# Where two of eight three-operand products stand in a graph kernel's second block

## The chip, the cores and the metric

The kernel runs on one core of a Trainium2 chip. The metric is the device time in microseconds (us) of one execution. The profile is one execution recorded by the hardware profiler; its times start at the first recorded instruction.

## The reference, cut to what matters

Four layers follow each other on 256 nodes of 512 features: a graph diffusion, a mixture of experts, a graph layer with 64 paths, and a second layer of experts. The change is in the third one, which works on 4352 edges:

```python
x1 = x_nodes[src].reshape(-1, N_SEG, EXTENT)          # 16 segments of 32
x2 = x_edges.reshape(-1, N_SEG, EXTENT)
i1, i2, i3 = (path_indices[:, 0], path_indices[:, 1], path_indices[:, 2])
contrib = path_coeffs[None, :, None] * x1[:, i1, :] * x2[:, i2, :]
edge_out = jnp.zeros(...).at[:, i3, :].add(contrib)
out = jnp.zeros((n_nodes, OP_SIZE), x_nodes.dtype).at[dst].add(edge_out.reshape(-1, OP_SIZE))
```

So each of 64 paths takes one segment of the gathered node rows, one segment of the edge rows and a coefficient, and adds the product to one segment of the edge's output. The outputs are then added up by target node.

## The kernel before

The 4352 edges lie as 34 tiles of 128, and they are taken in three blocks of 10, 14 and 10 tiles. In a block the 64 paths run one after the other. The running number of a path is n = 64 b + p, with b the block and p the path.

Each path passes three engines. ScalarE scales the path's edge segment by its coefficient into one of 12 slots (`scale(n)`, L595). VectorE multiplies the slot in place by the gathered node segment (`multiply(n)`, L1011). Then the slot is used up by two engines: TensorE adds the first tiles of it into PSUM (8 in the first block, 6 in the second, 4 in the third) by a matmul with the identity (L1326, L1329), and VectorE adds the remaining tiles into SBUF (`add(n)`, L1021). The counters are `scaled`, `mults`, `psums` and `sums`, in this order. A slot is written again 12 paths later, so `scale(n)` waits for `psums` and `sums` to reach n - 11.

The order on VectorE is written out by hand: multiply(n+1), add(n), multiply(n+2), and so on, over all three blocks without a break.

For paths with `direct(b, p)` true, which are paths 0 to 7 of the second block, ScalarE does nothing. VectorE makes the product out of three operands (segment of the node rows, coefficient, segment of the edge rows) with one `scalar_tensor_tensor` (L1006).

At the end of a block TensorE closes its PSUM banks (L1337, `block_ps`). ScalarE copies the eight banks of the first block out (`copy_sums`, L605 and L610, `block_out`), and TensorE opens them again for the next block, each when its copy is done (L1317, with two small matmuls, L1319, behind each). On ScalarE the copies of the first block stand in the queue ahead of its first work for the second block, which is scale(72).

TensorE also adds the finished tiles of the previous block into the nodes (`scatter`, L1273 and L1276), one tile after every sixth path of the second block. ScalarE makes the matrices for that (L573). After the last of these, ScalarE clears room for the third block (L627) and then scales its first paths.

GpSimd gathers the node rows of the third block by indirect DMAs, one per tile (L460). It waits until VectorE has made 64 products in all, then one product more for each third path. Their landings are counted in `row_in`, for which VectorE waits at the first product of a block.

Segment numbers are data. They lie packed in registers, and each engine computes a path's numbers from a word by a division and a remainder. At block changes words are moved to other registers (`moved`, `move_word`, L240).

Of the kernel before, what the change touches and what calls it, by code (L numbers as in the profile page):

```python
# [5 lines left out]
def graph_and_experts(nc, x, src, dst, edge, gnn_w, gnn_b, diff_w, wr, br, wgate, bgate,  # L6
# [37 lines left out]
    ROW_PATHS = -(-NP // 3)  # L44
# [8 lines left out]
    OWN_SLOTS, XN_SLOTS, PART_SLOTS = 5, 2, 3  # L53
    DR = 5
    BEHIND = 14
    DIRECT = [0, 8, 0]
    FREE_SLOTS = 2
    SPLIT = 8
    KEPT_AT = BLOCKS[2] - KEPT[2] - (BLOCKS[2] - SPLIT)
# [5 lines left out]
    with ExitStack() as ctx:  # L65
# [3 lines left out]
        def sem(name):  # L69
            return ctx.enter_context(nc.semaphore(name))  # L70
# [77 lines left out]
        def slot(n):  # L148
            return slots[n % SLOTS]

        def direct(b, p):

            return p < DIRECT[b]

        take = carve(big[:, :])
        w_sb = take([KC, D])
# [71 lines left out]
        def load_words(engine, lo, n):  # L228

            regs = [engine.alloc_register(f"{engine.engine.name}_word{load_words.made + i}") for i in range(n)]  # L230
            load_words.made += n
            engine.load(regs, path_w[0:1, lo:lo + n])
            return [engine.snap(r, donate=True, min_val=0, max_val=NS ** 6 - 1) for r in regs]
        load_words.made = 0

        def moved(engine, value, top):

            reg = engine.alloc_register(f"{engine.engine.name}_moved{load_words.made}")
            load_words.made += 1
            engine.reg_mov(reg, value)  # L240
            return engine.snap(reg, donate=True, min_val=0, max_val=top)

        def move_word(engine, words, i):
            words[i] = moved(engine, words[i], NS ** 6 - 1)
# [11 lines left out]
        def segment(ap, seg):  # L256

            b = ap.bitcast(mybir.dt.uint8).rearrange("p t (s u) -> p t s u", u=4 * U)
            return b[:, :, bass.ds(seg, 1), :].rearrange("p t o u -> p t (o u)").bitcast(mybir.dt.float32)

        def first_column(words, p):
            return column(words[p % ROW_PATHS], 2 * (p // ROW_PATHS))
# [4 lines left out]
        def single_column(words, p):  # L267
            return column(words[p // 6], p % 6)
# [13 lines left out]

        scatter_tile = {n: t for b in range(NB) for n, t in scatter_order(b)}
        split_tiles = [t for _, t in scatter_order(NB - 1)][BLOCKS[NB - 1] - SPLIT:]

        def gather_bank(t):
# [24 lines left out]
        edge_in = [sem(f"edge_in{b}") for b in range(NB)]  # L311
# [175 lines left out]
        def _(act):  # L487
# [67 lines left out]
            words = load_words(act, ROW_PATHS, COL_PATHS)  # L555
# [15 lines left out]
            def one_hot(n):  # L571
                act.wait_ge(scattered, n - DR + 1)
                nc.scalar.activation(dst_oh[:, n % DR, :], dst_ohb[:, scatter_tile[n], :], ACT.Copy).then_inc(dst_made, 1)  # L573

            def scattered_at(n):
                b = max(i for i in range(NB) if FIRST[i] <= n)
                return NP * (b + 1) + scatter_paths(b + 1)[n - FIRST[b]]

            def scale(n):
                b, p = n // NP, n % NP  # L580
                if p == DIRECT[b]:
                    act.wait_ge(edge_in[b], 16 if b < NB - 1 else 16 * (BLOCKS[b] // 2))
                if b and (p % 6 == 0 or p == DIRECT[b]):
                    move_word(act, words, p // 6)

                if n == FREE_SLOTS:
                    act.wait_ge(xn_out, 16 * H)
                if n == FREE_SLOTS + XN_SLOTS:
                    act.wait_ge(part_r, 2 * H)
                if n == OWN_SLOTS + XN_SLOTS:  # L590
                    act.wait_ge(gat_ps, PE_TILES)
                if n >= SLOTS:
                    act.wait_ge(psums, n + 1 - SLOTS)
                    act.wait_ge(sums, n + 1 - SLOTS)
                nc.scalar.activation(slot(n)[:, 0:BLOCKS[b], :],  # L595
                                     segment(edges[:, FIRST[b]:FIRST[b] + BLOCKS[b], :], single_column(words, p)),
                                     ACT.Copy, scale=coef_b[:, p:p + 1]).then_inc(scaled, 1)

            def copy_sums(b, lo, hi):
                if b >= 2:  # L600
                    act.wait_ge(scattered, FIRST[b - 1])
                for i, q in enumerate(sum_banks(b)[lo:hi], lo):
                    act.wait_ge(block_ps, banks_before(b) + i + 1)
                    if i < PT:
                        nc.scalar.activation(  # L605
                            kept_sums[b][:, 0:PT, i * P:(i + 1) * P].rearrange("p t (k u) -> p k t u", u=U),
                            bank[q].rearrange("p (k t u) -> p k t u", t=PT, u=U), ACT.Copy).then_inc(block_out, 1)
                    else:
                        w = D // PT2[b]
                        nc.scalar.activation(  # L610
                            kept_sums[b][:, PT:KEPT[b], (i - PT) * w:(i - PT + 1) * w].rearrange("p t (k u) -> p k t u", u=U),
                            bank[q].rearrange("p (k t u) -> p k t u", t=PT2[b], u=U), ACT.Copy).then_inc(block_out, 1)
# [3 lines left out]
            for n in range(FREE_SLOTS + XN_SLOTS):  # L616
                scale(n)
            for t in range(0, PE_TILES, 2):
                copy_gathered(t)
            for n in range(FREE_SLOTS + XN_SLOTS, NP * NB):  # L620
                b, p = n // NP, n % NP
                if b == 1 and p == 0:
                    copy_sums(0, 0, 8)
                if b == 2 and p == 0:
                    act.wait_ge(scattered, FIRST[1])
                    for i in range(BLOCKS[b] - KEPT[b]):
                        nc.scalar.activation(rest_sums[b][:, i, :], zero_b[:, 0:1].broadcast_to([P, D]), ACT.Copy)\  # L627
                            .then_inc(cleared[b], 1)
                for m in range(DR, T - SPLIT):
                    if scattered_at(m - DR) + BEHIND == n:  # L630
                        one_hot(m)
                if not direct(b, p):
                    scale(n)
                if b == 2 and p == LEAD - 1:
                    copy_sums(1, 0, PT)
                if b == 2 and p == REST_LEAD - 1:
                    copy_sums(1, PT, 8)
# [71 lines left out]
        def _(dve):  # L709
# [266 lines left out]

            nc.vector.memset(rest_sums[1][:, 0:4, :], 0.0).then_inc(cleared[1], 1)
            dve.wait_ge(packed, 3)
            words = [load_words(dve, 0, ROW_PATHS + -(-max(DIRECT) // 6))]
            for t in range(1, PE_TILES, 2):  # L980
                dve.wait_ge(gat_ps, t + 1)
                nc.vector.tensor_copy(x1g[0][:, t, :], gather_bank(t)).then_inc(gathered_odd, 1)  # L982
# [3 lines left out]
            def multiply(n):  # L986
                b, p = divmod(n, NP)
                if b and p < ROW_PATHS:
                    words[b][p] = moved(dve, words[b - 1][p], NS ** 6 - 1)
                if b and p % 6 == 0 and direct(b, p):  # L990
                    words[b][ROW_PATHS + p // 6] = moved(dve, words[b - 1][ROW_PATHS + p // 6], NS ** 6 - 1)
                tiles, xg = BLOCKS[b], x1g[b % 2]
                if p == 0:
                    if b == 0:
                        dve.wait_ge(gathered, PE_TILES // 2)
                        dve.wait_ge(row_in[b], 16 * (tiles - PE_TILES))
                    else:
                        dve.wait_ge(row_in[b], 16 * tiles)
                    if direct(b, 0):
                        dve.wait_ge(edge_in[b], 16)  # L1000
                v = slot(n)[:, 0:tiles, :]
                if direct(b, p):
                    if n >= SLOTS:
                        dve.wait_ge(psums, n + 1 - SLOTS)
                    i2 = single_column(words[b][ROW_PATHS:], p)
                    nc.vector.scalar_tensor_tensor(  # L1006
                        out=v, in0=segment(xg[:, 0:tiles, :], first_column(words[b], p)), scalar=coef_b[:, p:p + 1],
                        in1=segment(edges[:, FIRST[b]:FIRST[b] + tiles, :], i2), op0=ALU.mult, op1=ALU.mult).then_inc(mults, 1)
                    return
                dve.wait_ge(scaled, sum(not direct(*divmod(m, NP)) for m in range(n + 1)))  # L1010
                nc.vector.tensor_tensor(v, segment(xg[:, 0:tiles, :], first_column(words[b], p)), v, ALU.mult).then_inc(mults, 1)  # L1011

            def add(n):
# [7 lines left out]
                nc.vector.tensor_tensor(v, v, slot(n)[:, KEPT[b]:BLOCKS[b], :], ALU.add).then_inc(sums, 1)  # L1021

            multiply(0)
            for n in range(NP * NB):
                if n + 1 < NP * NB:
                    multiply(n + 1)
                add(n)
# [441 lines left out]
```

## Time and profile before

| | |
|---|---|
| three runs | 277.69, 277.73, 277.73 us; median 277.73 |
| the profiled execution | 277.7 us |
| its span | 275.9 us |
| granted TensorE clock in it | 1.00 of full speed |
| busy: TensorE matmul, VectorE, ScalarE, GpSimd | 96%, 82%, 60%, 23% of the span |

The span runs from the first to the last recorded instruction; 1.8 us of the execution's time lie around it. PE is TensorE's matmuls, PEld its weight loads, DVE VectorE, ACT ScalarE, POOL GpSimd. A q behind an engine's name is its sequencer, which handles register work. TensorE's busy share says little by itself, since overlapping matmuls that keep the engine warm are counted too.

### The profile page before, as it was taken

What the parts mean: (1) busy time and instruction counts of PE and PEld (TensorE: products, weight loads), DVE (VectorE), ACT (ScalarE), POOL (GpSimd) and SP (SyncE); (2) the same over time, 40 slices, a digit from 0 to 9 for tenths busy, and PEclk for the clock granted to TensorE, in tenths of its full rate; (3) what the DMA queues carried; (4) which work ended last, traced back from release to release, by engine and by line L of the source; (5) the groups of instructions that cost most, each with busy time, mean ns of one, the idle gap of its engine ahead of it and who ended that gap; (6) DMA issues with size and microseconds to landing.
All of it is one profiled execution on the core that took longest, in us unless ns stands there. A gap on an engine that the chain in (4) does not pass through costs nothing.

```text
span 275.9 us, 5689 instructions
## 1 busy us (share of the span) xinstructions
PE 265.6 (96%) x1651; PEld 186.7 (68%) x1660; DVE 224.9 (82%) x662; ACT 165.8 (60%) x336; POOL 63.1 (23%) x52
## 2 busy tenths in 40 slices
PE   6999999999999899999999999989999999999996
PEld 4666698886444799997778786756666664468633
DVE  5977565199657999999999999999999987855372
ACT  6920451011526999945788788499988819552260
POOL 4000060060006644304669991000000000000000
PEclk9999999999999999999999999999999999999999
DMA  5799990000014657733250002013544429000002
GB/s 186 242 412 410 442 406 17 0 2 1 1 38 128 179 137 254 223 119 86 66 131 26 2 1 76 4 24 150 159 151 148 154 86 349 27 0 2 2 0 76
DMA packets 12592, 33.91 MB, mean 123 GB/s; under 512 B 3345, under 2 KB 3602, under 8 KB 12306
## 3 DMA queue, kind: packets, MB, share of 16 engines
q1 hardware_dynamic: 10482, 26.73, 26.9%
q0 software_dynamic: 2080, 6.82, 8.6%
q8 instruction: 14, 0.23, 0.4%
q14 instruction: 16, 0.13, 0.2%
HBM read 32.50 MB, written 1.05 MB: 122 GB/s over the span
## 4 chain that ended last, share of the span: by engine, by line
PE 80%; DVE 9%; ACT 6%; issue 3%; DVEq 1%; DMA 1%; ACTq 0%; SPq 0%
PE psum L1326 15%; PE psum L1276 12%; PE psum L1230 10%; PE psum L1329 8%; PE psum L1254 5%; PE psum L1259 4%; PE psum L1402 3%; PE psum L1428 3%; PE psum L1173 3%; DVE big L1021 2%; PE psum L1159 2%; PE psum L1282 2%; PE psum L1317 2%; PE psum L1182 1%; PE psum L1440 1%
## 5 line engine op out<-in xcount | busy, mean ns | idle before, releaser
L460 POOL DMA_INDIRECT big<-xn_rows,big x26 | 51.3, 1974 | 54.5 <-DMA xn_rows<-xn 23.4
L595 ACT ACTIVATE prod<-edges,coef_b 128x320 f32 (+1 forms) x77 | 43.0, 593 | 10.1 <-PE psum L1329 8.4
L1276 PE MATMUL psum<-big,dst_oh 128*128 128x512 f32 x104 | 48.8, 593 | 0.0
L1011 DVE TENSOR_TENSOR prod<-big,prod 128x320 f32<-128x320 f32 (+1 forms) x77 | 40.5, 527 | 0.4 <-DVE big L982 0.2
L1326 PE MATMUL psum<-prod,ident 128*128 128x128 f32 x160 | 32.0, 294 | 0.6 <-DVE prod L1011 0.5
L1326 PEld LDWEIGHTS psum<-prod,ident 128*128 128x128 f32 x160 | 24.4, 190 | 10.0 <-issue 9.1
L1230 PE MATMUL psum<-edges,big 128*128 128x256 f32 x128 | 28.3, 380 | 0.0
L1276 PEld LDWEIGHTS psum<-big,dst_oh 128*128 128x128 f32 x104 | 18.0, 191 | 13.5 <-issue 13.4
L1230 PEld LDWEIGHTS psum<-edges,big 128*128 128x128 f32 x128 | 24.1, 190 | 3.5 <-issue 0.3
L1021 DVE TENSOR_TENSOR big<-big,prod 128x64 f32 (+2 forms) x80 | 26.3, 328 | 0.1
L595 ACT ACTIVATE xparts<-edges,coef_b 128x320 f32 (+1 forms) x45 | 24.2, 584 | 1.1 <-PE psum L1326 0.9
L1011 DVE TENSOR_TENSOR xparts<-big,xparts 128x320 f32<-128x320 f32 (+1 forms) x45 | 23.5, 523 | 0.3 <-ACT xn L595 0.3
L1329 PE MATMUL psum<-prod,ident 128*128 128x64 f32 (+1 forms) x110 | 19.8, 262 | 0.0
L1326 PE MATMUL psum<-xparts,ident 128*128 128x128 f32 x96 | 19.1, 294 | 0.7 <-DVE xparts L1011 0.7
L595 ACT ACTIVATE xn<-edges,coef_b 128x320 f32 (+1 forms) x32 | 17.6, 589 | 0.4 <-PE psum L1326 0.2
L551 ACT ACTIVATE edges<-psum 128x256 f32<-128x256 f32 x8 | 3.1, 384 | 24.2 <-PE psum L1230 18.6
L1011 DVE TENSOR_TENSOR xn<-big,xn 128x320 f32<-128x320 f32 (+1 forms) x32 | 16.8, 525 | 0.3 <-issue 0.2
L1329 PEld LDWEIGHTS psum<-prod,ident 128*128 128x128 f32 x110 | 16.7, 192 | 0.0
L595 ACT ACTIVATE src_t<-edges,coef_b 128x320 f32 (+1 forms) x30 | 16.3, 581 | 0.6 <-PE psum L1326 0.6
L1326 PEld LDWEIGHTS psum<-xparts,ident 128*128 128x128 f32 x96 | 14.1, 190 | 2.9 <-issue 2.6
L1021 DVE TENSOR_TENSOR big<-big,xparts 128x192 f32 (+2 forms) x48 | 15.9, 331 | 0.2 <-issue 0.2
L1011 DVE TENSOR_TENSOR src_t<-big,src_t 128x320 f32<-128x320 f32 (+1 forms) x30 | 15.6, 519 | 0.0
(217 smaller groups left out, 501.1 us busy)
## 6 DMA issues: line engine op xcount, KB each, us to landing
big<-in_w SPq DMA_DIRECT2D x3, 2048.0 KB, 16.2
edges<-in_f SPq DMA_DIRECT2D x11, 512.0 KB, 3.5
edges<-in_edge SPq DMA_DIRECT2D x1, 3584.0 KB, 23.9
edges<-in_edge SPq DMA_DIRECT2D x1, 2560.0 KB, 23.7
edges<-in_edge SPq DMA_DIRECT2D x5, 512.0 KB, 4.2
edges<-in_f SPq DMA_DIRECT2D x1, 2560.0 KB, 10.2
big<-in_gnn_w SPq DMA_DIRECT2D x1, 1024.0 KB, 6.3
xs<-in_x SPq DMA_DIRECT2D x1, 512.0 KB, 3.8
```

The lines of the kernel that those rows point to most:

```text
L460: nc.gpsimd.indirect_dma_start(out=x1g[b % 2][:, i, :], out_offset=None, in_=xn_rows, in_offset=bass.IndirectOffsetOnAxis(ap=idx_i[:, 0, F ...
L595: nc.scalar.activation(slot(n)[:, 0:BLOCKS[b], :], segment(edges[:, FIRST[b]:FIRST[b] + BLOCKS[b], :], single_column(words, p)), ACT.Copy, ...
L1011: nc.vector.tensor_tensor(v, segment(xg[:, 0:tiles, :], first_column(words[b], p)), v, ALU.mult).then_inc(mults, 1)
L1021: nc.vector.tensor_tensor(v, v, slot(n)[:, KEPT[b]:BLOCKS[b], :], ALU.add).then_inc(sums, 1)
L1173: last = mm(bank[2 + h], xnT[:, kc, h * P:(h + 1) * P], w_sb[:, kc, :], start=kc == 0, stop=kc == KC - 1)
L1230: last = mm(bank[2 + c % 4][:, n * N:(n + 1) * N], w[:, kc, c * P:(c + 1) * P], xnT[:, kc, :], start=kc == 0, stop=kc == KC - 1)
L1254: last = mm(bank[2 + h], hT[:, c, h * P:(h + 1) * P], w2_sb[:, c, :], start=c == 0, stop=c == HC - 1)
L1259: last = mm(gather_bank(t), src_t[:, h, t * P:(t + 1) * P], xparts[:, k, h, :], start=h == 0 and k == 0, stop=h == H - 1 and k == 2)
L1276: last = mm(bank[2 + h], dst_oh[:, n % DR, h * P:(h + 1) * P], tile_sums(b, t), start=False, stop=False)
L1326: last = mm(path_sums(to), ident[:], product[:, 0:PT].rearrange("p t u -> p (t u)"), start=False, stop=False, skip_group_check=True)
L1329: last = mm(more_sums(b, to), ident[:], product[:, PT:KEPT[b]].rearrange("p t u -> p (t u)"), start=False, stop=False, skip_group_check=True)
L1402: last = mm(bank[2 + k][64 * j:64 * j + 64, i * P:(i + 1) * P], yT[:, kc, c, :], f1_sb[:, kc, c * P:(c + 1) * P], start=k > 0 and kc == 0, ...
```

## The change

Paths 0 to 5 of the second block are no longer direct: ScalarE scales them and VectorE multiplies with two operands. Paths 6 and 7 stay direct. ScalarE's copies of the first block's sums move behind the scales of paths 0 to 5, so that its order is scale(63), scale(64) to scale(69), the eight copies, scale(72). The wait for the edge rows of the second block stands ahead of scale(64) on ScalarE and ahead of path 6 on VectorE.

```diff
-    DIRECT = [0, 8, 0]
+    DIRECT_LO, DIRECT_HI = 6, 8
 
         def direct(b, p):
 
-            return p < DIRECT[b]
+            return b == 1 and DIRECT_LO <= p < DIRECT_HI
 
             def scale(n):
                 b, p = n // NP, n % NP
-                if p == DIRECT[b]:
+                if p == 0:
                     act.wait_ge(edge_in[b], 16 if b < NB - 1 else 16 * (BLOCKS[b] // 2))
-                if b and (p % 6 == 0 or p == DIRECT[b]):
+                if b and (p % 6 == 0 or b == 1 and p == DIRECT_HI):
                     move_word(act, words, p // 6)
 
             for n in range(FREE_SLOTS + XN_SLOTS, NP * NB):
                 b, p = n // NP, n % NP
-                if b == 1 and p == 0:
+                if b == 1 and p == DIRECT_LO:
                     copy_sums(0, 0, 8)
 
-            words = [load_words(dve, 0, ROW_PATHS + -(-max(DIRECT) // 6))]
+            words = [load_words(dve, 0, ROW_PATHS + -(-DIRECT_HI // 6))]
 
-                    if direct(b, 0):
-                        dve.wait_ge(edge_in[b], 16)
                 v = slot(n)[:, 0:tiles, :]
                 if direct(b, p):
+                    if p == DIRECT_LO:
+                        dve.wait_ge(edge_in[b], 16)
                     if n >= SLOTS:
                         dve.wait_ge(psums, n + 1 - SLOTS)
```

## Rows read from the trace of the kernel before

**Rows 1.** Windows of VectorE: stretch, time, busy time (count), clock, DMA

```profile
133.31:182.37 49.06, 48.95 (x114) 1.00 0.14 38
182.37:226.00 43.63, 43.15 (x129) 1.00 0.41 137
```

**Rows 2.** Timeline, VectorE, at the first block change: start, length, engine, line, operation

```profile
125.16 0.21 DVE L1021 TENSOR_TENSOR big<-big,prod 128x64 f32 x1
125.29 0.48 DVE L1011 TENSOR_TENSOR xn<-big,xn 128x320 f32<-128x320 f32 x1
125.70 0.21 DVE L1021 TENSOR_TENSOR big<-big,xn 128x64 f32 x1
126.05 0.69 DVE L1006 SCALAR_TENSOR_TENSOR prod<-big,coef_b,edges 128x448 f32 x1
```

**Rows 3.** The same timeline through the direct paths and behind them

```profile
126.79 0.68 DVE L1006 SCALAR_TENSOR_TENSOR prod<-big,coef_b,edges 128x448 f32 x1
...
133.31 0.61 DVE L1011 TENSOR_TENSOR prod<-big,prod 128x448 f32<-128x448 f32 x1
...
137.67 0.61 DVE L1011 TENSOR_TENSOR prod<-big,prod 128x448 f32<-128x448 f32 x1
138.35 0.43 DVE L1021 TENSOR_TENSOR big<-big,prod 128x256 f32 x1
...
163.96 0.61 DVE L1011 TENSOR_TENSOR src_t<-big,src_t 128x448 f32<-128x448 f32 x1
164.60 0.43 DVE L1021 TENSOR_TENSOR big<-big,src_t 128x256 f32 x1
```

**Rows 4.** VectorE's sequencer by line: count, ns min/median/max, first and last start

```profile
L1011 DVEq FUSED_REGOPS  x184: 93/140/164, 90.4 to 225.1; - x184
L1006 DVEq FUSED_REGOPS  x8: 178/210/242, 125.8 to 131.9; - x8
```

**Rows 5.** Timeline, ScalarE, at the first block change

```profile
120.43 0.56 ACT L595 ACTIVATE xn<-edges,coef_b 128x320 f32 x1 [0.15 <-PE psum L1329]
126.94 2.07 ACT L605 ACTIVATE big<-psum 128x512 f32<-128x512 f32 x4 [5.94 <-remote]
130.78 1.29 ACT L595 ACTIVATE prod<-edges,coef_b 128x448 f32 x2
```

**Rows 6.** Timeline, TensorE: last path of the first block, an early scatter, three late ones

```profile
126.30 0.39 PE L1329 MATMUL psum<-xn,ident 128*128 128x128 f32 x2
138.08 1.88 PE L1276 MATMUL psum<-big,dst_oh 128*128 128x512 f32 x4
165.47 1.88 PE L1276 MATMUL psum<-big,dst_oh 128*128 128x512 f32 x4
170.75 1.88 PE L1276 MATMUL psum<-big,dst_oh 128*128 128x512 f32 x4
175.98 1.88 PE L1276 MATMUL psum<-big,dst_oh 128*128 128x512 f32 x4
```

**Rows 7.** Timeline, ScalarE and VectorE, at the second block change

```profile
177.90 3.22 ACT L627 ACTIVATE big<-zero_b 128x512 f32<-128x512 bf16 x6 [3.13 <-PE psum L1276]
181.03 1.00 ACT L595 ACTIVATE xparts<-edges,coef_b 128x320 f32 x2
182.37 0.49 DVE L1011 TENSOR_TENSOR xparts<-big,xparts 128x320 f32<-128x320 f32 x1
```

**Rows 8.** Timeline, GpSimd: four of the ten gathers for the third block

```profile
128.67 0.95 POOL L460 DMA_INDIRECT big<-xn_rows,big  x1 [0.38 <-DVE prod L1006]
134.19 4.91 POOL L460 DMA_INDIRECT big<-xn_rows,big  x1 [1.79 <-DVE prod L1011]
144.81 20.58 POOL L460 DMA_INDIRECT big<-xn_rows,big  x1 [1.19 <-DVE prod L1011]
165.69 1.03 POOL L460 DMA_INDIRECT big<-xn_rows,big  x1 [0.30 <-DVE prod L1011]
```

**Rows 9.** The gathers' line by itself: time from issue to landing

```profile
DMA to landing us min/median/max: 3.5/3.7/5.3
```

## The prediction

> **What bounds the kernel now.** The page's busy shares come first, and they mislead here: TensorE is busy for 96% of the span, and the chain that ended last goes through it over most of the path loops. So I read the windows of VectorE next. From the first two-operand product of the second block to the first product of the third it is busy for 48.95 of 49.06 us, and from there to the end of the loops for 43.15 of 43.63 us [rows 1]. Its timeline shows no wait for another engine in these two stretches. TensorE by itself is faster: in the second block its scatters, one in six paths, start 4.56 us apart while it has a backlog (27.39 us for six of them, from 138.08 to 165.47) [rows 6], and VectorE's six paths last 6 x 0.872 = 5.23 us [rows 3]. TensorE begins the block late and so looks full, but it has caught up by the scatter at 170.75, which comes 5.28 us after the one before, 0.72 us later than TensorE's own pitch would have it. From there it waits for VectorE. So VectorE's queue sets the time from 125.3 us to the end of the loops at 226 us, and behind that the tail runs as one serial chain. What shortens VectorE's queue anywhere in the second block is worth its full length, up to the 0.72 us that TensorE has in hand at that scatter.
>
> **The change part by part.** *Six products with two operands.* The direct product at 126.79 and the two-operand one at 133.31 are seven paths apart, 6.52 us or 0.931 us a path. The two-operand products at 133.31 and 137.67 are five paths apart, 4.36 us or 0.872 us a path [rows 3]. Both pitches hold the same addition. Six paths change: 6 x 0.059 = 0.355 us less. This is the main term. Paths 6 and 7 stay as they are.
>
> The Trainium skill ("VectorE: DVE Perf Modes", section "The TRN2 errata — SBUF-src ops pay a fixed extra latency per instruction") gives VectorE's time by a fixed part and the element count alone; by that both forms would last the same and this term would be nothing. The trace differs: 0.68 us against 0.61 us for the same 128x448 [rows 3]. The measurement decides, and the rule has no chance of its own.
>
> *The head of the block.* In the first block a product starts 0.13 us after the start of the addition ahead of it (125.16 to 125.29). The first product of the second block starts 0.35 us after it (125.70 to 126.05), so 0.22 us are lost there [rows 2]. The engine has no wait on another one; it is the sequencer, whose register work for a direct product lasts 210 ns against 140 ns for the other [rows 4], and which moves one word more. With a two-operand product first, 0.07 us of register work and the extra move go. Bounds: nothing, if the new wait for `scaled` takes as long as what it replaces, and the whole 0.22 us. I take 0.10, by the 0.07 us of the median rows and a little for the move. At path 6, where the move and the longer register work now stand, they have the 0.87 us of a product and an addition ahead of them as cover, as they had on the direct paths 1 to 7; uncovered they would cost the same 0.10 us again.
>
> *Six scales more on ScalarE.* It starts scale(63) at 120.43 us and then stands idle for 5.94 us until the copies at 126.94 [rows 5]. Scale(64+k) needs `psums` at 53+k. TensorE finishes path 63 at 126.30 + 0.39 = 126.7 us [rows 6], and one path each 0.54 us before that (125.16 to 125.70 on VectorE, which sets that pace) [rows 2]. So the last scale may start at 126.7 - 6 x 0.54 = 123.5 us and ends by 124.2, as two of them take 1.29 us [rows 5]. The first product that needs one is due at 126, and the first copy at 126.94. The cover is 2.7 us; if it were gone, each further 0.1 us would reach the copies, then TensorE's opening of the banks, and only beyond the 0.72 us of slack above the end. What is queued behind the new waits is the copies on ScalarE, and TensorE waits for these. Cost taken: nothing.
>
> *The wait for edge rows* moves to ScalarE at about 121 us. The transfers from outside that fill these rows are issued in the kernel's first 30 us, and VectorE finds them there at 126 without a wait [rows 2]; I take nothing, and no wait is added that anyone sees. The word moves on ScalarE are one register instruction more, in idle time: nothing.
>
> *What is queued behind.* All later steps are counted from VectorE's products: TensorE's last scatter of the second block (175.98), ScalarE's clearing behind it (177.90), scale(128) at 181.03, which VectorE needs at 182.37 [rows 6, 7]. These shift with VectorE, and so do the transfers that SyncE issues by `mults`. Scale(128) ends by 181.6, so there is 0.8 us of room as well. In the third block VectorE is idle for 0.48 us in 43.63 [rows 1], so nothing takes the gain up.
>
> *Sum.* 0.355 + 0.10 = 0.455 us. The profiled execution took 277.7 us, its span 275.9; that gives 277.25 us, and against the median of 277.73 it gives 277.3 us, a saving of 0.16%.
>
> **The rivals.** *Rival A: GpSimd is shut out, and the third block waits for its rows (slower).* Most gathers last 0.95 to 1.1 us, but two of those that start under VectorE's two-operand products of the second block last 4.91 and 20.58 us [rows 8]. Both begin after a wait for one of these products, and both end about 0.75 us after VectorE has a pause between a product and its addition: 138.35 stands 0.68 us behind its product, where the others have 0.53, and 164.60 is the second such place [rows 3]. The gather at 128.67, which waits for a direct product, lasts 0.95 us. After the change this one starts under two-operand products too, and may be held. A held gather costs nothing by itself: the last one is issued at 165.69 and lands 3.7 us later [rows 8, 9], and its rows are due at 182.0. It decides when a gather is still open behind the pause near 164 us and is then held until VectorE itself stops at the first product of the third block. Price: 0.75 us from the pause to the end of the issue and 3.7 us for the landing, 4.5 us, all of it on VectorE's full queue: 277.3 + 4.5 = 281.8 us; with two gathers open a further 1.3 us. Against it: each gather that followed straight after a held one got through, and the phases behind path 8 stay the same relative to VectorE. The Trainium skill ("SBUF — State Buffer", section "Who interferes with whom") says that a VectorE instruction with two SBUF inputs contends with a GpSimd instruction that reads SBUF; both product forms have two, so by it the change would add no exposure, while the rows above show a difference between places only.
>
> *Rival B: the time goes down by less than 0.1 us, or not at all.* VectorE has a pause of 0.1 to 0.2 us about every 30 paths, where its sequencer seems to fetch. The shorter code in front shifts the places of these pauses; if one lands where there is less cover, as in the first block's short additions or at the head of the second block, it takes up to 0.2 us, and the uncovered register work at path 6 the other 0.10: 277.45 to 277.75 us. For it speaks that the gain is so small; against it, that the pauses in the second block were 0.14 and 0.10 us and can hardly grow.
>
> *Rival C: more is gained.* The head's whole 0.22 us goes, and a pause is hidden: 0.355 + 0.22 + 0.10 = 0.68 us, 277.05 us. TensorE's 0.72 us of slack lets it through.
>
> *Rival D: the six scales hold up the copies.* It would need 2.7 us of delay, for instance by edge rows that come late; nothing in the profile shows it. 278 us or more.
>
> **How the numbers follow.** A difference of about 0.2% (0.56 us) is what a measurement of this kernel can tell from no change; faster begins below 277.17 us and slower above 278.29. The forecast, 277.3 us with a range of its own from 277.1 to 277.45, has 0.64, of which 0.12 lies below 277.17. Rival B has 0.13, rival C 0.10, rival A 0.09, rival D and other ways to be slower 0.04. So faster has 0.12 + 0.09 (nearly all of C) = 0.21, slower 0.12 (A, and most of D), within 0.2% the rest, 0.67. The range for 8 in 10 holds the forecast, B and C: 277.0 to 277.8.
>
> **What would show each step right or wrong.** In the profile after: six products on L1011 from about 125.95 us at a pitch of 0.87 us, then two on L1006 at 0.93; path 8 at 132.85 instead of 133.31. On ScalarE six scales between 121 and 124.3 us, copies still at 126.94. TensorE's first products of the block still at 130.85, and its scatters up to 165.5 unmoved, then everything earlier by 0.45 us. No wait of VectorE at the first product of the third block; a wait for a transfer there is rival A. Copies after 127 us are rival D. The head of the block still 0.35 us behind its addition would make the head term wrong. A total that is lower by 0.45 us at path 8 and not at the end of the loops would make the claim wrong that VectorE's queue sets the time.

## The result: slower by 1.4%

| | before | after |
|---|---|---|
| median | 277.73 us | 281.53 us (281.40 to 281.68) |
| profiled execution, span | 277.7, 275.9 us | 281.57, 279.8 us |
| busy: TensorE, VectorE, ScalarE, GpSimd | 96, 82, 60, 23% | 96, 80, 60, 29% |

The ratio is 1.0137, with a 95% interval from 1.0124 to 1.015. The kernel was forecast at 277.3 us, inside 277.0 to 277.8. It came out 0.27 us below where rival A had it, at 281.8 us.

The page's busy shares are the first hint: only GpSimd's has grown, from 23 to 29% of the span. Its timeline in the profile of after, from the third gather for the third block on, answers to [rows 8] (start, length, engine, line, operation, idle time before it with its releaser):

```profile
129.23 0.94 POOL L460 DMA_INDIRECT big<-xn_rows,big  x1 [0.30 <-DVE xparts L1011]
...
133.76 5.25 POOL L460 DMA_INDIRECT big<-xn_rows,big  x1 [1.78 <-DVE prod L1011]
139.31 1.19 POOL L460 DMA_INDIRECT big<-xn_rows,big  x1 [0.30 <-issue]
...
144.34 38.34 POOL L460 DMA_INDIRECT big<-xn_rows,big  x1 [1.19 <-DVE prod L1011]
182.99 0.95 POOL L460 DMA_INDIRECT big<-xn_rows,big  x1 [0.30 <-issue]
```

The gather that lasted 20.58 us in the kernel before now lasts 38.34 us, and the tenth can only be issued at 182.99. VectorE's timeline of after, through the head of the second block, around 164 us and at the change to the third block, answers to [rows 2, 3, 7]:

```profile
125.71 0.23 DVE L1021 TENSOR_TENSOR big<-big,xn 128x64 f32 x1
125.93 0.63 DVE L1011 TENSOR_TENSOR prod<-big,prod 128x448 f32<-128x448 f32 x1
...
132.88 0.61 DVE L1011 TENSOR_TENSOR prod<-big,prod 128x448 f32<-128x448 f32 x1
...
164.36 0.61 DVE L1011 TENSOR_TENSOR prod<-big,prod 128x448 f32<-128x448 f32 x1
164.90 0.41 DVE L1021 TENSOR_TENSOR big<-big,src_t 128x256 f32 x1
...
181.44 0.41 DVE L1021 TENSOR_TENSOR big<-big,prod 128x256 f32 x1
186.78 0.49 DVE L1011 TENSOR_TENSOR xparts<-big,xparts 128x320 f32<-128x320 f32 x1 [4.92 <-DMA big<-xn_rows,big]
```

Around 164 us the addition follows its product after 0.54 us, as everywhere, where the kernel before took 0.64 us. VectorE is 0.43 us ahead at path 8 (132.88 against 133.31) and would have begun the third block at 181.78, 0.59 us ahead. There it waits 4.92 us for rows, and starts 5.00 us late. The chain that ended last goes through the same steps, one right behind the other (start, length, what):

```profile
144.34 38.34 POOL big L460
182.68 0.30 POOLq L65
182.99 3.61 DMA big<-xn_rows,big
```

ScalarE, which got the added work, does it as planned. Six scales run from 120.97 to 124.43 us, and the copies begin where they did:

```profile
120.97 1.79 ACT L595 ACTIVATE prod<-edges,coef_b 128x448 f32 x3
122.66 1.77 ACT L595 ACTIVATE xparts<-edges,coef_b 128x448 f32 x3
126.97 2.07 ACT L605 ACTIVATE big<-psum 128x512 f32<-128x512 f32 x4 [2.53 <-remote]
```

A table of places in VectorE's timeline, from the profiles (us; the last column is the end marked by the first statistics of the tail, L720):

```
kernel                                    path 8   third block   last addition   tail
before                                    133.31   182.37        226.44          240.31
after                                     132.88   186.78        230.31          244.18
after, gathers unpaced                    132.85   181.78        225.49          239.36
after, three records more                 133.05   182.10        226.18          240.04
before, one record more                   133.45   192.30        235.98          249.85
```

The tail is the same length in each of them (13.87 us from the last addition). So all of the difference is in VectorE's queue.

### The profile page after: what moved, and what is told of

It reads as the page before. It is cut to its first block, busy times and chain, and to the rows that moved or that the text cites. A ratio compares the mean times of both kernels' runs of the same rounds, so it can differ in the third digit from the quotient of the medians.

```text
span 279.8 us, 5705 instructions
## 1 busy us (share of the span) xinstructions
PE 268.1 (96%) x1651; PEld 187.8 (67%) x1660; DVE 224.7 (80%) x662; ACT 168.2 (60%) x342; POOL 81.4 (29%) x52
## 4 chain that ended last, share of the span: by engine, by line
PE 67%; POOL 14%; DVE 9%; ACT 4%; issue 2%; DMA 2%; DVEq 1%; ACTq 0%; SPq 0%; POOLq 0%
POOL big L460 14%; PE psum L1326 11%; PE psum L1230 10%; PE psum L1276 8%; PE psum L1329 5%; PE psum L1254 5%; PE psum L1259 4%; PE psum L1402 3%; PE psum L1428 3%; PE psum L1173 2%; PE psum L1159 2%; DVE big L1021 2%; PE psum L1282 2%; PE psum L1182 1%; DMA big<-xn_rows,big 1%
## 5 line engine op out<-in xcount | busy, mean ns | idle before, releaser
L460 POOL DMA_INDIRECT big<-xn_rows,big x26 | 69.6, 2678 | 53.3 <-DMA xn_rows<-xn 23.5
L595 ACT ACTIVATE prod<-edges,coef_b 128x320 f32 (+1 forms) x80 | 44.4, 593 | 11.4 <-PE psum L1329 9.7
L1276 PE MATMUL psum<-big,dst_oh 128*128 128x512 f32 x104 | 50.1, 607 | 0.0
L1011 DVE TENSOR_TENSOR prod<-big,prod 128x320 f32<-128x320 f32 (+1 forms) x80 | 42.3, 530 | 0.2 <-DVE big L982 0.2
L1011 DVE TENSOR_TENSOR xparts<-big,xparts 128x320 f32<-128x320 f32 (+1 forms) x48 | 25.4, 530 | 5.2 <-DMA big<-xn_rows,big 4.9
L595 ACT ACTIVATE xparts<-edges,coef_b 128x320 f32 (+1 forms) x48 | 25.7, 586 | 1.4 <-PE psum L1326 1.3
L1326 PE MATMUL psum<-xparts,ident 128*128 128x128 f32 x96 | 19.7, 297 | 2.5 <-DVE xparts L1011 2.5
```

Source lines behind the costliest of these rows:

```text
L460: nc.gpsimd.indirect_dma_start(out=x1g[b % 2][:, i, :], out_offset=None, in_=xn_rows, in_offset=bass.IndirectOffsetOnAxis(ap=idx_i[:, 0, F ...
L595: nc.scalar.activation(slot(n)[:, 0:BLOCKS[b], :], segment(edges[:, FIRST[b]:FIRST[b] + BLOCKS[b], :], single_column(words, p)), ACT.Copy, ...
L1276: last = mm(bank[2 + h], dst_oh[:, n % DR, h * P:(h + 1) * P], tile_sums(b, t), start=False, stop=False)
L1326: last = mm(path_sums(to), ident[:], product[:, 0:PT].rearrange("p t u -> p (t u)"), start=False, stop=False, skip_group_check=True)
```

## The experiments

Theory 1: a gather is held on GpSimd while VectorE runs two-operand products and additions without a pause; the change covered the pause near 164 us that had freed it. Theory 2: the time went elsewhere, into the moved scales and copies, and the wait for rows only shows it.

**The gathers unpaced.** In the changed kernel:

```diff
-                    if b == 2 and i >= 2:
-                        pool.wait_ge(mults, NP + 3 * (i - 1))
```

> The changed kernel, in which GpSimd no longer spreads its gathers for the third block over VectorE's products: all ten follow each other once 64 products are made. Theory 1 (one gather is held by GpSimd until VectorE pauses, and the third block waits 4.9 us for its rows): the gathers end before 145 us, VectorE does not wait at its first product of the third block, and the time is 276.9 to 277.3 us. A rule that the held gather is chance alone would allow one long record here too, without a wait if it ends before 178 us. Theory 2 (the time went into the moved scales and copies, and the wait only shows it): 281 us or more, unchanged.

Measured: 276.76 us (276.75 to 276.77 in six executions), ratio 0.9966 [0.9954, 0.9979]. Slightly below the expected range. Here is GpSimd's timeline, the last five gathers:

```profile
133.12 5.85 POOL L458 DMA_INDIRECT big<-xn_rows,big  x1 [0.30 <-issue]
139.28 1.18 POOL L458 DMA_INDIRECT big<-xn_rows,big  x1 [0.30 <-issue]
140.77 0.94 POOL L458 DMA_INDIRECT big<-xn_rows,big  x1 [0.30 <-issue]
142.02 1.10 POOL L458 DMA_INDIRECT big<-xn_rows,big  x1 [0.30 <-issue]
143.42 0.94 POOL L458 DMA_INDIRECT big<-xn_rows,big  x1 [0.30 <-issue]
```

One gather is held here as well, for 5.85 us, until 0.83 us after a pause of 0.07 us near 138.15, and it costs nothing, since all are done by 144.4. All of the loss is gone with ScalarE's and VectorE's part of the change in place. Theory 2 is out.

**The last two gathers left out.** In the changed kernel:

```diff
-                for i in range(0 if b else PE_TILES, BLOCKS[b]):
+                for i in range(0 if b else PE_TILES, BLOCKS[b] - (2 if b == 2 else 0)):
-                        dve.wait_ge(row_in[b], 16 * tiles)
+                        dve.wait_ge(row_in[b], 16 * (tiles - (2 if b == 2 else 0)))
```

> The changed kernel without the last two gathers of the third block (tiles 8 and 9 keep the first block's rows, so part of the gather is left out) and without the wait for them. It gives what the wait for these rows costs by itself. Theory 1: no wait at the third block and 277.0 us, that is the 0.6 us that VectorE's queue was ahead at that point. Theory 2: 281 us or more, or a wait of VectorE for something else at the same place.

Measured: 276.69 us, ratio 0.9963 [0.9949, 0.9977], 0.3 us below the forecast for it, and no wait at the third block. The wait for these two tiles is worth 281.53 - 276.69 = 4.84 us. It also says, as the run before, that the change itself is worth 1.0 us and not 0.46; more on that below.

**Half of the change.** `DIRECT_LO` is 3, so that paths 3 to 7 stay direct, and VectorE also moves their word at path 3.

> The change by half: paths 3 to 7 of the second block are direct, only paths 0 to 2 are scaled by ScalarE, ahead of its copies. Theory 1 (whether a gather is held past the second block depends on where VectorE's pauses fall): one of two outcomes, near 277.5 us with no wait at the third block (a saving of 3 x 0.059 us and the head's 0.1), or near 281.7 us with one; nothing between. Theory 2 (each replaced path costs something): about half way, 279.6 us.

Measured: 277.30 us (277.28 to 277.32), ratio 0.9986 [0.9975, 0.9996]. One of the two outcomes, with a gather held from 144.55 for 20.92 us, and the next one issued at 165.77. It is not half way. But the pause that frees this one is hardly to be seen:

```profile
164.23 0.41 DVE L1021 TENSOR_TENSOR big<-big,src_t 128x256 f32 x1
164.58 0.63 DVE L1011 TENSOR_TENSOR prod<-big,prod 128x448 f32<-128x448 f32 x1
```

The step from the addition to the product is 0.35 us where the others are 0.33 or 0.34. The trace keeps whole nanoseconds: this step is 346, and the other ones during this hold are 334 to 338. In the changed kernel's hold of 38.34 us the same steps are 334 to 336, and those from a product to its addition 534 to 537. So about 0.01 us more seems to be enough; the hold ends 0.89 us after it, and the one in the kernel before ends 0.78 us after its pause at 164.60.

**Empty instructions, twice without any.** Two edits of the changed kernel put 16 register moves ahead of path 40, and five empty instructions ahead of path 2.

> The changed kernel with 16 register moves on VectorE's sequencer ahead of its product of path 40 in the second block, near 161 us; nothing else. Theory 1 (a held gather goes on as soon as VectorE has a short pause): the gather that starts near 144 us ends within 1 us of this pause, near 162 us, the last gather follows, no wait at the third block, and the time is that of the shortened queue plus the pause, 277.2 to 277.6 us. Theory 2 (the gather is held for another reason, or must be started anew): its record still ends near 182 us and the time stays at 281.5 us or goes up by the pause.

> The changed kernel with five empty instructions on VectorE's queue ahead of its product of path 2 in the second block, as many as the change took out of this queue. Theory 1a (the places of VectorE's short pauses go by the position in its instruction stream, and the change moved one of them near 164 us to where it is covered): the pause of 0.02 to 0.1 us near 164 us is back, the gather that starts near 144.3 us ends near 165 us, and the time is 276.7 to 277.2 us. Theory 1b (the pause went for another reason, for instance since ScalarE does the scaling): the gather is held to 182 us and the time stays at 281.5 us.

Measured: 281.53 and 281.55 us, with the gather held from 144.33 for 38.34 us in both. The traces hold none of the added instructions: VectorE has 1120 records in both, as in the changed kernel. So these two runs are repeats of it, and they could not test what they were made for. They show that the hold comes back to 0.01 us, and nothing more.

**A short wait on VectorE.** In the changed kernel, in `multiply`:

```diff
+                if n == NP + 40:
+                    dve.wait_ge(psums, NP + 38)
```

> The changed kernel in which VectorE waits, ahead of its product of path 40 in the second block (160.9 us), until TensorE has used path 37, which happens at about 161.0 us. Theory 1: this makes a pause of 0.1 to 0.4 us near 161 us, the held gather ends within 1 us of it, the last gather follows, VectorE does not wait at the third block, and the time is 276.8 to 277.3 us, though an instruction is added that only waits. Theory 2 (the gather isn't held by VectorE's lack of pauses): record until 182 us and 281.5 us or more. If no pause shows in the timeline, the run tells nothing.

Measured: 277.45 us, ratio 0.9990 [0.9980, 0.9999], 0.15 us above the expected range: an instruction that only waits makes the changed kernel 4.1 us faster. VectorE's and GpSimd's timelines:

```profile
160.43 0.42 DVE L1023 TENSOR_TENSOR big<-big,prod 128x256 f32 x1
161.12 0.63 DVE L1013 TENSOR_TENSOR xparts<-big,xparts 128x448 f32<-128x448 f32 x1 [0.28 <-PE psum L1331]
```

```profile
144.23 17.44 POOL L460 DMA_INDIRECT big<-xn_rows,big  x1 [1.19 <-DVE prod L1013]
161.97 0.95 POOL L460 DMA_INDIRECT big<-xn_rows,big  x1 [0.30 <-DVE xparts L1013]
```

The pause is 0.35 us long, up to 161.12, and the held gather ends at 161.67.

**The place of the pauses.** Why had the pause gone? Counting all records of VectorE, its sequencer's among them, the pauses that no other engine causes stand at records 448, 575 or 576, 703 or 704, 832 and 960: 128 apart, in every kernel. The third of them is the one near 164 us. A path without moved words takes four records (register work, product, register work, addition). How long a pause is depends on which of the four it meets:

```
kernel                                records   pause at record 704
before; the same with gathers unpaced    1123   0.10; 0.13 us
after, three records more                1123   0.15
after, path 40 direct too                1122   0.04
half of the change                       1122   0.01
after, short wait (gather freed before)  1121   0.01
none direct, gathers unpaced             1118   0.02
after; the same with gathers unpaced     1120   none
before, one record more                  1124   none
```

The changed kernel has three records fewer, since the direct products needed more register work. That turned an open place into a covered one.

The profile also tells what comes every 128 records. Its queue q14 of instruction transfers moves packets of 8,192 bytes, though not only at these places. In the kernel before such packets start at 119.31, 139.02, 165.28, 189.47 and 209.13 us, each 0.67 to 0.71 us behind VectorE's record 448, 576, 704, 832 or 960. Behind record 704 one starts in all fourteen traces, 0.60 to 0.69 us later, whether there is a pause or not. So the places go with the loading of instructions; that the loading makes the pauses is likely, but not tested. The load by itself does not free a gather: in the changed kernel it starts at 165.09, and the hold goes on.

Two runs test whether the number of records decides, with increments of a counter that nobody reads; four of them make three records more in the built program, and two make one.

```diff
+                if n == NP + 2:
+                    for _ in range(4):
+                        dve.sem_inc(spare, 1)
```

> The changed kernel with three more instructions on VectorE's queue ahead of its product of path 2 in the second block (increments of a counter that nobody reads), so that the queue from there on is as long as in the kernel before. VectorE's pauses stand at records 448, 575, 703, 832 and 960 of its queue in all runs so far, 128 apart. Theory 1 (the change moved the place at 704 from an open to a covered one by taking three instructions out): the pause of 0.1 us near 164 us is back, the gather that starts at 144.3 us ends near 165 us, no wait at the third block, and 277.1 to 277.3 us (the third block's pauses are those of the kernel before too). Theory 2 (the pause went for another reason): 281.5 us.

Measured: 277.40 us, ratio 0.9989 [0.9979, 0.9999], 0.1 us above the expected range. The pause is back, the gather from 144.55 lasts 20.57 us as in the kernel before, and the last one is issued at 165.43:

```profile
163.67 0.64 DVE L1015 TENSOR_TENSOR src_t<-big,src_t 128x448 f32<-128x448 f32 x1
164.35 0.42 DVE L1025 TENSOR_TENSOR big<-big,src_t 128x256 f32 x1
```

> The kernel before with one more instruction of that kind at the same place, and nothing of the change. The two-operand paths take four records of the queue each, so one more stands to the pattern as three less. Theory 1: the pause near 164 us is covered as in the changed kernel, the gather that starts near 144.8 us is held until VectorE stops at the third block, and the time is 281.7 to 282.2 us. Theory 2 (the hold to 182 us needs ScalarE's moved scales or copies, or the two-operand products at the head): 277.7 us, as before.

Measured: 287.20 us, ratio 1.0339 [1.0322, 1.0357]. It is the kernel before with one record more and nothing of the change, and it is 9.5 us slower. I had expected 4 us. The pause at record 576 is covered too, so that the gather from 134.34 is held all the way, with five gathers behind it:

```profile
134.34 48.77 POOL L461 DMA_INDIRECT big<-xn_rows,big  x1 [1.79 <-DVE prod L1015]
183.41 0.95 POOL L461 DMA_INDIRECT big<-xn_rows,big  x1 [0.30 <-issue]
...
188.42 0.95 POOL L461 DMA_INDIRECT big<-xn_rows,big  x1 [0.30 <-issue]
```

```profile
192.30 0.49 DVE L1015 TENSOR_TENSOR xparts<-big,xparts 128x320 f32<-128x320 f32 x1 [10.00 <-DMA big<-xn_rows,big]
```

The arithmetic is that of the changed kernel with four gathers more: 10.00 us of wait against 4.92, and 4 x 1.25 = 5.0 us for the four. So the long hold needs neither ScalarE's scales nor the new order of its queue nor the two-operand products at the head. The same kind of instruction at the same place made the changed kernel 4.1 us faster and this one 9.5 us slower, so it is the count that decides and not the instruction.

**What unpacing is worth by itself.** The same edit in the kernel before:

> The kernel before, with all ten gathers of the third block following each other once 64 products are made, as in the run of the changed kernel with the same edit. Theory 1 (a held gather costs nothing as long as it ends in time): 277.7 us, no difference, so that the changed kernel's 276.76 us with this edit is the change's own gain of 0.9 us. Rival (part of that 0.9 us came from the gathers): 277.2 us or less here, and the change's own gain is the 0.46 us of the forecast.

Measured: 277.76 us, ratio 1.0001 [0.9991, 1.0010]. Nothing. So the 0.92 us of the changed kernel with unpaced gathers are the change's.

**None direct.** `DIRECT_LO` and `DIRECT_HI` are 8, gathers unpaced.

> All eight paths are scaled by ScalarE ahead of its copies, no direct product is left, and the gathers follow each other without pacing. The last scale needs TensorE at path 60 and may start at 124.6 us, so the copies still start at 126.95. By the pitches: 2 x 0.059 = 0.12 us less than the run with six paths and the same gathers, 276.65 us. If ScalarE's eight scales reach the copies, TensorE opens its banks later, and the time is 276.8 us or more.

Measured: 277.48 us, ratio 0.9991 [0.9981, 1.0001]; slower than with six paths by 0.7 us, and 0.8 us above the forecast. VectorE begins the third block at 181.82, no earlier than with six (181.78), though path 8 is at 132.79 against 132.85: its pauses at 576 and 704 are 0.15 and 0.02 us, against 0.07 and none. In the third block it has larger pauses at 832 and 960 (0.28 and 0.24 us against 0.12 and 0.06). From the last addition to the end of the span it takes another 0.36 us more, and that is one step in the tail. It stands at VectorE's record 1088, which is 960 + 128, and a packet of instructions starts 0.64 us behind it here too. The product there waits longer, with eight paths and then with six:

```profile
246.11 0.29 DVE L1046 SCALAR_TENSOR_TENSOR big<-tie,psum 128x128 f32<-128x128 f32 x1 [1.38 <-PE psum L1356]
245.38 0.29 DVE L1046 SCALAR_TENSOR_TENSOR big<-tie,psum 128x128 f32<-128x128 f32 x1 [1.01 <-PE psum L1356]
```

So the 0.7 us against six paths lie at these places. The scales did not reach the copies: TensorE's second path of the block starts at 131.26 us with six paths and at 131.28 with eight.

**Unpaced, with three records more.** The changed kernel with both edits.

> The changed kernel with unpaced gathers and the three more instructions. Theory 1 (of the 0.9 us by which the run with unpaced gathers is faster than the kernel before, 0.46 come from the head and the products, and the rest from smaller pauses at the places that the shorter queue brought): 277.1 to 277.25 us. Rival (the pauses cost nothing, the products gave more than thought): 276.8 us, unchanged.

Measured: six of ten executions took 277.40 to 277.44 us and the other four 281.46 to 281.57. The six are 0.15 us or more above the range of theory 1 and far from the rival's 276.8. The added records cost 0.25 us at the head, which the range left out: path 8 is at 133.10 us in the profile below, against 132.85 without them. With that they fit theory 1. The four are another matter. In the profile of one of them VectorE starts two products 2 us late (136.29 to 138.69, 139.23 to 141.61), while no gather lasts over 1.2 us, and TensorE and ScalarE stand still as well:

```profile
136.29 0.41 DVE L1023 TENSOR_TENSOR big<-big,xn 128x256 f32 x1
138.69 0.63 DVE L1013 TENSOR_TENSOR prod<-big,prod 128x448 f32<-128x448 f32 x1 [1.98 <-issue]
139.23 0.42 DVE L1023 TENSOR_TENSOR big<-big,xn 128x256 f32 x1
141.61 0.63 DVE L1013 TENSOR_TENSOR prod<-big,prod 128x448 f32<-128x448 f32 x1 [1.96 <-ACT prod L594]
```

What stops all three is open.

**One direct path late.** In the changed kernel path 40 is direct as well:

```diff
-            return b == 1 and DIRECT_LO <= p < DIRECT_HI
+            return b == 1 and (DIRECT_LO <= p < DIRECT_HI or p == 40)
```

> The changed kernel with path 40 of the second block made direct as well, in the middle of the stretch in which the gather is held; its three-operand product stands near 160.9 us. Theory 1 (only a pause of VectorE lets the gather go, whatever the form of its instructions): if the sequencer's longer work for this product is covered, the gather is held on, to the pause near 164 us if the two added records open it, else to 182 us and 281.5 us. Theory 3 (a three-operand product itself lets GpSimd through): the gather ends by 162 us with no pause in front of it, no wait at the third block, and 276.8 to 277.5 us.

Measured: 277.14 us, ratio 0.9979 [0.9969, 0.9988]. VectorE and GpSimd:

```profile
160.56 0.42 DVE L1021 TENSOR_TENSOR big<-big,prod 128x256 f32 x1
160.89 0.68 DVE L1006 SCALAR_TENSOR_TENSOR xparts<-big,coef_b,edges 128x448 f32 x1
161.49 0.41 DVE L1021 TENSOR_TENSOR big<-big,xparts 128x256 f32 x1
```

```profile
144.35 17.44 POOL L460 DMA_INDIRECT big<-xn_rows,big  x1 [1.20 <-DVE prod L1011]
162.10 3.23 POOL L460 DMA_INDIRECT big<-xn_rows,big  x1 [0.30 <-issue]
```

The held gather ends at 161.79, 0.9 us after the three-operand product began, and there is no pause in front of it (0.33 us from the addition to the product, as everywhere). So theory 1 was too narrow: a pause frees the gather, and so does a path with one three-operand product. What in this path does it is not shown. Besides the form, the product is 0.06 us longer than the others, the addition behind it comes 0.06 us later than usual (0.60 us after the product), and the sequencer has more register work. The next gather is held too, for 3.23 us. It ends at 165.33, 0.86 us after a pause of 0.04 us at record 704.

## Why the prediction was wrong

**The step that failed** is the one in rival A that gave it 0.09: "the phases behind path 8 stay the same relative to VectorE". The gathers' starts do stay the same, 144.34 against 144.81 with VectorE 0.43 us ahead. The pause that ended the hold does not. It goes by the record number, and the change took out three. Rival B said in plain words that the shorter code shifts the pauses, and priced that as a cost of 0.2 us to VectorE; that GpSimd lives on these pauses stood in rival A. I never put the two together. Together they would have made rival A likelier than 0.09. In the sum, the wait for rows at the third block had no term at all; it measured 4.92 us.

**Rival A's mechanism and price** were right: 4.5 us forecast, 4.92 us waited. The 0.4 us left out are 0.3 us between the end of the held gather and the start of the last one, and that the hold ended 0.90 us after VectorE's next product was due (181.78 to 182.68), not 0.75. That its total of 281.8 us comes so close to 281.53 is in part luck. Against the run with unpaced gathers the wait is worth 281.53 - 276.76 = 4.77 us, so the price was 0.3 us too low, and the 277.3 us under it was 0.5 us too high. What it said on the third gather came out otherwise: that one, now under two-operand products, lasted 0.94 us. It was the ninth that decided.

**The products.** From 125.93 to 132.88 us are 6.95 us, against 126.05 to 133.31, 7.26 us: 0.31 us. Six of eight steps were to give 0.355; one step took 0.05 us longer, up to the addition at 129.81, beside a gather. Right.

**The head.** 0.22 us from the addition to the product against 0.35 before, 0.13 less where 0.10 was taken. Right.

**ScalarE.** Six scales, done at 124.4, copies at 126.97, TensorE's first products where they were. Right: nothing.

**The sum.** 0.43 us at path 8, as forecast (0.455, with 132.85 named). But the unhindered change gave 0.92. The rest is pauses. Rival B had them only as a loss, of 0.1 to 0.2 us each, where they reach 0.27 us in the third block, and rival C hid one: the ones at records 576 and 704 went from 0.15 + 0.10 to 0.07 us, and in the third block (181.78 to 225.49 against 182.37 to 226.44) 0.36 us are gone, most of it at records 832 and 960, where 0.27 and 0.27 became 0.12 and 0.06. The run with three records more gets the third block's part back, at 44.08 us against 43.71 and 44.07 before. So the term "pauses" was sized at nothing and was larger than the one for the products. Rival C's direction was right and its 277.05 us still 0.3 too high.

**The claim on the bound** held: VectorE's lead and its wait both came through to the end of the loops in full.

**The Trainium skill.** Its page "SBUF — State Buffer", section "Who interferes with whom", has two-input VectorE instructions contend with GpSimd ones that read SBUF, and infers that `tensor_tensor` does not stall the making of descriptors. Here gathers that GpSimd issues stood for up to 48.77 us beside a stream of two-operand instructions. That speaks against the inference, though no run shows that the descriptors are what stood still. The rule of two inputs does not tell either which gathers are held, nor why one path with a three-operand instruction, which has two tensor inputs as well, let one go. The Trainium skill's "Runtime: NRT & Kernel Launch", section "Instruction fetch mechanics", has instructions come in blocks of 16 KiB, or 256 instructions, and the fetch hidden by the sequencer's pace. Here packets of 8,192 bytes follow every 128 records of VectorE's path loops, and VectorE loses up to 0.32 us at these places. So size and period are half of the page's, and if the fetch is what makes the pauses, it is not always hidden.

## What to carry to other kernels

Where GpSimd issues gathers beside a VectorE queue that never pauses, look at the longest record of a gather, not at the mean, and ask what ended it; if it was chance, the kernel's time hangs on the count of instructions in another queue, and one more of them cost 9.5 us here. Issue such gathers early enough that a hold ends in time, or give VectorE a short wait or, as in one run here, a three-operand instruction in between, and time such a kernel over small shifts of its code before believing a change of 0.3%. The fastest kernel that computes the whole reference was the change with unpaced gathers, 276.76 us, though its variant with three records more shows that unpaced gathers can meet another stall.

## What the runs showed of the hardware that I had not expected

A gather's issue, mostly 0.94 to 1.1 us and at most 1.6 when it gets through, can be held beside VectorE's stream for as long as that stream has no pause (3, 5, 17, 21, 38 and 49 us in these runs), while its neighbours in the same stream pass. One ended 0.89 us after a step that was only 0.01 us longer than the others. VectorE in turn lost only 0.04 to 0.05 us to some of the gathers that got through.

VectorE pauses at every 128th record of its queue, by nothing to 0.36 us, as the covering work allows, and a packet of instructions of 8,192 bytes starts 0.60 to 0.71 us behind most of these records.

What decides whether a gather is held at its start is not settled. In the kernel before, the two held ones started on a wait for a product; in the changed kernel with unpaced gathers one was held that followed straight on another.
